# Where the halves of the attention result are formed: ScalarE and VectorE straight from PSUM, in place of an fp32 copy and a GpSimd subtraction

## What is computed

```python
q = hidden_states @ _dequant(q_codes, q_scales)      # 32 heads of 128
k = hidden_states @ _dequant(k_codes, k_scales)      # 8 groups of 128
v = hidden_states @ _dequant(v_codes, v_scales)
q = _rope(q); k = _rope(k)                           # k, v repeated 4 times
scores = jnp.einsum('bhqd,bhkd->bhqk', q, k) * scale + mask[None, None]
attn = jax.nn.softmax(scores, axis=-1)
out = jnp.einsum('bhqk,bhkd->bhqd', attn, v)
return out @ _dequant(o_codes, o_scales)

x = x + _layernorm(attention(_layernorm(x)))
x = x + _layernorm(ffn(_layernorm(x)))               # silu(gate) * up, then down
```

## Time and profile before

| | |
|---|---|
| median of 3 runs | 1483.3 us (1478.01 to 1486.79) |
| the profiled execution, its own time | 1479.83 us |
| its span, first to last instruction | 1478.0 us |
| mean granted TensorE clock | 0.985 |
| busy, share of the span: TensorE matmul | 94% |
| VectorE | 75% |
| ScalarE | 67% |
| GpSimd | 67% |

### The profile page before, as it was taken

How to read it: one execution, slowest core, us unless ns; L and a number is a source line. 1 busy time by engine, 2 the same in 40 slices (tenths; PEclk the granted TensorE clock), 3 DMA queues, 4 the chain that set the end, 5 groups by cost and what they waited for, 6 DMA issues and landing times.

```text
span 1478.0 us, 33061 instructions
## 1 busy us (share of the span) xinstructions
PE 1386.7 (94%) x10944; PEld 837.3 (57%) x10944; DVE 1115.5 (75%) x2480; ACT 987.1 (67%) x2582; POOL 996.5 (67%) x710
## 2 busy tenths in 40 slices
PE   3689999999999999999999999999999968999998
PEld 1455665656656666666666665666666643454543
DVE  7856787777777878777777877788878795686744
ACT  2468777777777878877877887778777853241321
POOL 2369888888878888888888888888888751010100
PEclk9899999999999999999999999999999988999999
DMA  7389999999998998998899989899999854011000
GB/s 231 80 171 173 172 173 179 171 189 178 186 171 180 170 177 171 171 174 165 166 167 180 173 171 172 172 169 187 175 165 179 154 104 81 16 43 51 8 30 29
DMA packets 523323, 217.09 MB, mean 147 GB/s; under 512 B 479280, under 2 KB 481424, under 8 KB 523152
## 3 DMA queue, kind: packets, MB, share of 16 engines
q1 hardware_dynamic: 520592, 210.74, 72.9%
q0 software_dynamic: 2560, 4.23, 1.7%
HBM read 55.44 MB, written 4.29 MB: 40 GB/s over the span
## 4 chain that ended last, share of the span: by engine, by line
PE 63%; SPq 10%; DMA 9%; issue 6%; POOL 4%; DVE 4%; ACT 3%; POOLq 0%; DVEq 0%; ACTq 0%
DMA ot<-o_parts 7%; PE ps_p L848 6%; PE ps_p L849 6%; PE ps_p L873 5%; PE ps_p L874 5%; PE ps_p L851 5%; PE ps_s L1083 4%; PE ps_s L1082 4%; SPq L419 4%; PE ps_s L888 3%; PE ps_s L886 3%; PE ps_s L887 3%; PE ps_o L904 3%; PE ps_o L902 3%; PE ps_o L903 3%
## 5 line engine op out<-in xcount | busy, mean ns | idle before, releaser
L546 POOL TENSOR_TENSOR p_lo<-prob,p_hi 128x1280 f16<-128x1280 f32 x128 | 335.9, 2624 | 113.2 <-ACT p_hi L695 91.6
L1208 DVE SCALAR_TENSOR_TENSOR y<-ps_p,wo_scale,y 128x512 f32<-128x512 f32 x512 | 380.5, 744 | 32.8 <-PE ps_p L874 32.2
L686 ACT ACTIVATE prob<-prob,exp_bias 128x512 f32<-128x512 f32 (+3 forms) x512 | 285.5, 558 | 12.4
L1221 DVE CUSTOM_DVE_ANT_0 prob<-ps_s,mask 128x512 f32<-128x512 f32 (+3 forms) x512 | 236.7, 482 | 39.0 <-PE ps_s L888 38.6
L848 PE MATMUL ps_p<-x_hi,w_hi 128*128 128x512 f16 x640 | 244.5, 382 | 5.5 <-DVE w_lo L1108 3.9
L849 PE MATMUL ps_p<-x_lo,w_hi 128*128 128x512 f16 x640 | 244.4, 382 | 0.0
L873 PE MATMUL ps_p<-ot,wo 128*128 128x512 f16 x512 | 197.6, 386 | 36.7 <-DMA ot<-o_parts 27.6
L902 PE MATMUL ps_o<-v_hi,ffn_w 128*128 128x128 f16 x1280 | 221.8, 219 | 0.0
L903 PE MATMUL ps_o<-v_lo,ffn_w 128*128 128x128 f16 x1280 | 221.8, 219 | 0.0
L904 PE MATMUL ps_o<-v_hi,ffn_w 128*128 128x128 f16 x1280 | 221.7, 219 | 0.0
L530 POOL TENSOR_TENSOR rot<-rot,swap 128x512 f32<-128x512 f32 x160 | 202.6, 1275 | 24.8 <-DMA swap<-other 24.7
(11 more groups left out here) (113 smaller groups left out, 2945.7 us busy)
## 6 DMA issues: line engine op xcount, KB each, us to landing
swap<-other SPq DMA_DIRECT2D x320, 128.0 KB, 2.8
w_code<-w_codes SPq DMA_DIRECT2D x36, 384.0 KB, 3.5
w_scale<-scratch SPq DMA_DIRECT2D x36, 384.0 KB, 5.2
o_code<-o_codes SPq DMA_DIRECT2D x35, 256.0 KB, 3.1
swap<-x SPq DMA_DIRECT2D x16, 256.0 KB, 2.8
out<-z SPq DMA_DIRECT2D x16, 256.0 KB, 2.0
ffn_w<-x SPq DMA_DIRECT2D x3, 1024.0 KB, 9.5
ffn_w<-p_hi SPq DMA_TRANSPOSE x128, 3.7
```

What stands on the lines that cost most here:

```text
L546: pool.tensor_tensor(p_lo[:, :], prob[:, hp, :], p_hi[:, :], ALU.subtract).then_inc(p_lod, 1)
L686: act.activation(prob[:, hp, a:a + w], prob[:, hp, a:a + w], ACT.Exp, bias=exp_bias[:, hp, i:i + 1], scale=-1.0, accum_out=exp_sum[:, hp, ...
L1208: dve.scalar_tensor_tensor(tile, ps_p[:, bank, :], scale, tile, ALU.mult, ALU.add).then_inc(o_add, 1)
L1221: dve.tensor_tensor_reduce(prob[:, hp, P_AT[i]:P_AT[i] + w], ps_s[:, bank, col:col + w], mask[:, S - w:], -SCORE_SCALE, NO_MINIMUM, ALU.ad ...
```

## The change

ScalarE's four scaled copies out of `ps_o` now write fp16 straight into `o_hi`; the fifth instruction and the buffer's use as an fp32 copy are gone, and the four wait for the transpose of the head before. `o_low` moves from GpSimd to VectorE as four instructions of 128 columns that read `ps_o` and `o_hi` and write `ps_o` times the inverse sum minus `o_hi`. In VectorE's order they stand in each head behind the first output addition. `attend` now waits for these four. At the end VectorE has `o_low` of head 126 ahead of `rows_add(3)` and that of head 127 behind the next four additions, and GpSimd has neither.

```diff
             def turn_o(n, hp):
...
-                sp.wait_ge(oq_lod, n + 1)
+                sp.wait_ge(oq_lod, (n + 1) * TT)
...
-            def o_low(n):
-
-                after(pool, ot_in, 16 * n)
-                pool.sem_inc(pool_passed)
-                pool.wait_ge(oq_hid, n + 1)
-                pool.sem_inc(pool_passed)
-                pool.tensor_tensor(o_lo, o_f[:, :], o_hi, ALU.subtract).then_inc(oq_lod, 1)
...
-                        o_low(n - 2)
...
-            o_low(UNITS * HG - 2)
             power(2 * TT - 1)
-            o_low(UNITS * HG - 1)
...
                 act.wait_ge(oq_ps, n + 1)
                 act.wait_ge(inv_done, n + 1)
-                after(act, oq_lod, n)
+                after(act, ot_in, 16 * n)
                 for i in range(TT):
-                    act.activation(o_f[:, i * P:(i + 1) * P], ps_o[:, i * P:(i + 1) * P], ACT.Copy,
-                                   scale=inv_sum[:, h, i:i + 1]).then_inc(oq_norm, 1)
-                after(act, ot_in, 16 * n)
-                act.wait_ge(oq_norm, (n + 1) * TT)
-                act.activation(o_hi, o_f[:, :], ACT.Copy).then_inc(oq_hid, 1)
+                    act.activation(o_hi[:, i * P:(i + 1) * P], ps_o[:, i * P:(i + 1) * P], ACT.Copy,
+                                   scale=inv_sum[:, h, i:i + 1]).then_inc(oq_hid, 1)
...
-                after(pe, oq_norm, n * TT)
+                after(pe, oq_lod, n * TT)
...
+            def o_low(n):
+
+                h = n % HG
+                dve.wait_ge(oq_hid, (n + 1) * TT)
+                after(dve, ot_in, 16 * n)
+                dve.sem_inc(dve_passed)
+                for i in range(TT):
+                    at = slice(i * P, (i + 1) * P)
+                    dve.scalar_tensor_tensor(o_lo[:, at], ps_o[:, at], inv_sum[:, h, i:i + 1], o_hi[:, at],
+                                             ALU.mult, ALU.subtract).then_inc(oq_lod, 1)
...
                         out_tile(h, g)
+                        if g == 0 and n > 1:
+                            o_low(n - 2)
...
+            o_low(UNITS * HG - 2)
             rows_add(TT - 1)
             for nt in range(KT):
                 add_last(1, nt, nt)
+            o_low(UNITS * HG - 1)
             to_xn(TT - 1)
```

More of the change, by code:

```diff
@@ L319, in layer @@
         oq_ps = sem("oq_ps")
-        oq_norm = sem("oq_norm")
         oq_hid = sem("oq_hid")
@@ L1057, in _ @@
                 last_output(3, nt, (nt + 2) % RING)
-            pe.wait_ge(oq_norm, UNITS * HG * TT)
+            pe.wait_ge(oq_lod, UNITS * HG * TT)
             pe.wait_ge(ffn_in, 2 * KT * 16)
```

## The result

The changed kernel takes 1486.2 us (median of 17 runs, 1482.8 to 1491.6), the kernel before 1479.5 us on the same chip: a ratio of 1.0044, 95% interval 1.0033 to 1.0055. So it is slower by 0.44%: inside the 0.5% that I called no change and inside the range, but clear of its interval, on the slower side, and 4 us more than the +2 of my sum. The profiled spans differ by 6.3 us (1484.3 against 1478.0), and the profiles are compared with these.

What follows compares the result with a forecast made beforehand. TensorE was taken as the bound (1039.7 of 1060 us busy), held up by late `ot` transposes. Terms -8 + 7 + 3 - 2 + 2 = +2 us on 1479.8 gave 1482, predicted as 1483 us, range 1467 to 1501.

Steps and rivals of the forecast that it cites:

- Part 7: Pipeline fill -2 us; at the end VectorE's lateness +2 us, down-weight load ahead of last `ot` nothing (-2 to +3).
- Part 2: GpSimd loses `o_low`; `p_low`, `p_lo` and `ot` of head 2 come earlier: gain of 8 us, at most 15.3.
- Part 3: VectorE's four new 128-column instructions take 1.05 us a head at 0.26 us each; busy to 90%, not the bound.
- Parts 4 and 5: `p_hi` 1.05 us late, hitting head 0: 7 us loss (0 to 31); Q0's `other` 0.5 us late: 3 us (to 15).
- Part 6: `attend` waits for VectorE's `o_low` of the head before: costs nothing, with some 4 us of cover.
- Part 1: ScalarE loses one rounding, 0.63 us a head; behind a late `ot` its four copies add some 0.5 us, mostly covered.
- Faster through `w_lo`: VectorE's `w_lo` starts ahead of GpSimd's `p_low`, giving VectorE 1.8 us back in many units: about 1468 us, chance 0.30.
- Slower through SyncE's queue: Late `p_hi` and `other` reach `ot` in heads 0 and 1; TensorE waits 21 us more: 1501 us, chance 0.32.
- The signs I named: VectorE 88-91% busy, 0.26 us pitch, `p_hi` waits over 130 us, `ot` waits: none in head 3, more in 1-2.

Runs made afterwards that it cites:

- e6: Kernel before, with only the down-weight load waiting for the last `ot` transpose to land: 1474.3 us beside 1480.8 (0.9961).
- e1: Changed kernel, GpSimd waiting for head 1's `ot` transpose to land before each of eight gate and up loads: 1474.1 us (0.9978).
- e5: e1 with the down-weight load also waiting for the last `ot` transpose to land: 1466.0 us (0.9923 against the kernel before).
- e10: e5 with a GpSimd subtraction of `o_low`'s length in its old place, every head from unit 2, no added wait: 1469.4 us (0.9939).
- e9: e5 without VectorE's four `o_low` instructions, the low half left at zero: 1469.6 us (0.9924).
- e13: e5 with VectorE's `o_low` behind the second output addition instead of the first: 1482.8 us (1.0026).
- e2: Kernel before, with the same wait as e1 ahead of the same eight loads: 1486.8 us (1.0063).
- e3: Kernel before, the eight loads issued in head 3 right behind `p_low`, ahead of `o_low` and the `ot` transpose: 1492.4 us (1.0101).

## Why the prediction was right or wrong

I forecast no change, and the kernel got slower, clear of its interval. The time was only 3 us above my number, but that nearness is luck: it rests on terms of +12, -10 and +5 which my sum didn't have. By its parts:

**Part 7 failed, and it is the one that sets the sign.** It saw the down-weight load move ahead of the last `ot` and priced that "at nothing, with ends of -2 and +3". The transpose landed after 10.0 us instead of 8.3, and e6 shows that even the kernel before was paying 6.1 us there: its load was issued 0.15 us ahead of that `ot` already, not behind it, and I didn't look at its landing, but took the earlier trace rows, a median over 128, in which the slow ones don't show. Worse, the same question was never put for the eight loads in the steady part, behind `rope_add` in GpSimd's order. I listed what GpSimd would do earlier and followed computation only. Cost: +12.8 (e1; +9.3 by e5) and +2.4 of the end (8.5 - 6.1); without these two the profiled difference of +6.3 would be -8.9 (-5.4 by e5). Of its other two numbers, the fill (-2) came to -1.2 and VectorE's part of the end (+2) to +1.5, neither clear of what like kernels differ by. "A step that is moved" includes the ones that move because the instruction ahead of them is gone.

**Part 2: right in direction, wrong in size and in what it priced.** A gain in the steady part is there, at -9.8 us over twenty units, about -14 for the 29.4 (9.8 x 29.4/20), at the far end of "8 us, at most 15.3". I priced GpSimd's saved work at 1.26 us a head and saw its 40.9 us of waiting as an addition; e10 gives the work back for nothing, so the gain is of the wait, by the likeliest reading, or of ScalarE's lost rounding.

**Part 3: right as to the price.** Four instructions and the next piece:

```profile
322.08 0.75 DVE L1193 SCALAR_TENSOR_TENSOR y<-ps_p,wo_scale,y 128x512 f32<-128x512 f32 x1
322.74 1.12 DVE L1218 SCALAR_TENSOR_TENSOR o_parts<-ps_o,inv_sum,o_parts 128x128 f16<-128x128 f32 x4
323.77 0.55 DVE L1206 CUSTOM_DVE_ANT_0 prob<-ps_s,mask 128x384 f32<-128x384 f32 x1
```

(322.74 + 1.03 = 323.77, a pitch of 0.26 us; their group gives each 344 ns). VectorE's share came out lower than I said, 84.5%, mostly because each `w_lo` got 1.6 us shorter (2.44 to 0.80 on average over all 32). That it wasn't the bound, as part 3 said, e5 and e9 show: with and without its new work TensorE is busy 678.5 and 678.6 of the 680 us.

**Parts 4 and 5: direction right, price wrong.** `p_hi` is late and GpSimd waits for it, 248.6 us. I charged 7 + 3 us, with ends of 31 and 15. e9, with none of VectorE's new work, matches e5 in both steady stages (327.4 and 696.4 against 327.5 and 696.4); the fill (141.0 for 143.5) is within the spread, the end (55.5 for 57.1) is the 1.5 us above. Net of the shorter `w_lo` they cost nothing in the steady part. The cover I had in view, 1.8 us in head 1 and none in head 0, was read in one unit of a GpSimd that still had `o_low`; that GpSimd has the time without it is my reading.

**Part 6: right here, but the margin is narrower than told.** I wrote of "some 4 us" of cover for `attend`. At its place `o_low` costs nothing (e5 = e9), but one group of `lows` later it costs 1.0% (e13), by way of `ot` (24.1 us of waits from 120 to 460 and 480 to 1160 us, 12.1 in e5), which I hadn't tied to it.

**Part 1**: not tested by itself. Its condition, a late `ot` with the four copies behind it, came true: ScalarE waits 23.2 us for a landed `ot`, 20.7 of them from 120 to 460 us, where the loads are, and 10.7 there in e1. So it belongs to what the loads cost; its share isn't shown.

**The rivals.** *Faster through `w_lo`*: its condition came true in every unit; `w_lo` starts ahead of `p_low`, and takes 0.95 us at full width instead of 2.72:

```profile
328.17 0.95 DVE L1093 SCALAR_TENSOR_TENSOR w_lo<-w_scale,w_hi 128x768 f16<-128x768 f32 x1
```

That agrees with the rule of the Trainium skill (SBUF — State Buffer, section on SBUF's two separate sides): whoever starts first holds the port pair. `p_low`, which mostly starts 0.2 us behind it, pays with 3.2 us instead of 2.62 where it is held up. But the time I hung on it, 1468 us, didn't come, and e9 has the gain of the steady part without the short `w_lo`. What the 1.8 us are worth by themselves no run shows. *Slower through SyncE's queue*: the lateness I meant, of `p_hi` and `other`, passed through unseen; its sign of over 35 us in `ot` waits didn't show either (23.4 us). What did come through `ot` was late by its landing, not by its issue.

**The signs I named**: 0.26 us pitch yes; `p_hi` waits yes; VectorE 88 to 91% no; `ot` waits "grown in heads 1 and 2, with about the same sum" no: 22.0 of their 23.4 us stand before 460 us, where the loads are, and from 480 to 1160 us they are as good as gone (1.4 us in 5; 4.0 in 8 before). A table by stage was to be had before the prediction: the kernel before takes 36.1 us a unit with loads (324.5/9) and 35.3 without (706.1/20), a hint that the loads weren't free.

## What to carry to other kernels

When an instruction or a wait is taken out of an in-order engine, list everything that this engine then issues earlier, its loads first, and look at what lands beside them; a prefetch that nobody needs for a long time belongs behind the transfer that someone waits for, and whether its engine can afford that wait is to be measured (in the kernel before, e2, it cost 0.6%). On GpSimd here 1.28 us of added work a head cost nothing, and a wait at the same place 33 us of 696, so price the two apart. And cut the time by stage before believing that a small net difference means small effects.

## What the runs showed of the hardware

The `ot` transpose on SyncE's queue lands 3.2 us after its issue in the median, but 6.4 to 8.4 us after it when GpSimd's load of one gate or up row block went out 0.5 to 1.2 us ahead of it (eight cases in the changed kernel), 4.4 to 7.5 us when it went out 1.9 to 2.5 us ahead (e3), and 8.3 and 10.0 us beside the down-weight load (issued 0.15 and 2.9 us ahead). When the load went out 1.5 to 2.2 us behind the transpose, it landed after 3.1 us in six of eight cases, and after 3.5 and 4.3 in the other two. The wait that orders the down-weight load brings both kernels back to 3.1 us (e5, e6). A VectorE instruction over 128 PSUM columns shows 344 ns in its row but follows its predecessor after 0.26 us.
